# Look-up inputs by halves of the batch and two broadcast loads for the dense rows, in a one-core recommendation tower

## The chip, the core and the metric

The kernel runs on one core of a Trainium2 chip. The metric is the device time of one execution in microseconds, the median over runs. The core has a matrix engine (TensorE, PE in the rows), VectorE (DVE), ScalarE (ACT), GpSimd (POOL) and SyncE (SP), each with a program of its own; they wait for one another on semaphores. SyncE issues nearly all transfers, GpSimd the gathers, and all of them share 16 DMA engines.

## The reference

For 2048 rows the reference looks up 16 embeddings of 16 values in tables of 1,000 to 125,000 rows, forms products with 39 x 16 context values per row (r_x0), and contracts them with weights into z (16 x 16 values per row). A three-layer network follows.

```python
e = stack([tbl_s[ids[:, s]] for s in range(16)], axis=1)      # 2048 x 16 x 16
A = repeat(x0, s, axis=1)                                     # n = 16 * 39 pairs
Bm = repeat(xl, f, axis=2).reshape(b, s * f, d)               # xl is e
z = einsum('bnh,bnd,nk,khd,kd->bkh', A, Bm, alpha, w, hv)
h = concatenate([z, dense_ctx], axis=1)                       # 256 + 16 values
h = maximum(h @ W_top1 + b_top1, 0); h = maximum(h @ W_top2 + b_top2, 0)
y = h @ W_top3
```

## The kernel before, in words

**Look-ups.** Seven of the sixteen tables are gathered from memory by GpSimd (L340, indirect transfers of 128 rows each). The nine small ones (ONE_HOT, 1,000 or 1,250 rows) lie on chip and are looked up by matmuls. A row number is split in a low digit (0 to 249) and a high digit (0 to 3 or 4). `find_digits` computes both, ScalarE stores the low digits to the scratch tensor low_dram (L387), and SyncE's `load_low` brings them back broadcast to all 128 partitions in low_h. `make_onehot` (DVE) compares them with each partition's number, two instructions for one table, one for each half of the 250 low digits. `look_up` (PE) multiplies the one-hots with the table, which `split_tables` has split in three bf16 parts, into one of two banks of PSUM. `pick_rows` (DVE) masks the right high digit and sums, two instructions, into e_all. A unit is one table for one quarter of the batch (512 rows): 4 x 9 = 36 units, numbered i = 9u + n for quarter u and table n. Quarter 0 is looked up before the main loop, the others inside it.

**Main loop.** Eight groups of 256 rows, each with NC = 5 steps; step number = 5g + c. In each step DVE multiplies a 128 x 2048 block of x0 (x_main for steps c = 0 to 3, x_last for c = 4) with the spread and transposed embeddings (L585), and PE contracts the product with the coefficients (`contract`, L678). ScalarE spreads the embeddings of the next group (`spread_group`, L411), which needs all nine units of that pair of groups, and PE transposes them (L668). Inside group g PE also runs the network of group g-1: layer1 at steps c = 0 and 1 (L693, L699), layer2 at c = 2 (L709), layer3 at the end (L718).

**Order.** It is written out by hand. `units_at(step)` gives the units that are looked up in a step: UNITS_AT counts them over the ten steps of a pair of groups, and those are for the next pair. In PE's program a step is: its look-ups, its contraction, transposes and layers. In DVE's: the product, the picks of this step's units, the one-hots of the next step's. In ScalarE's program `round_dense` (which waits for all dense loads, dense_in) stands before `spread_group(0, 0)` and `copy_coef`; `split_dense` on DVE follows the ninth pick and waits for the rounding.

**Dense rows.** The 16 dense values and a row of ones (for the bias), padded to 32 rows of 2048 values, are needed four times, once for each block of 32 partitions, and w1d (32 x 512) likewise. They are staged in x0_last's second buffer and in z_sb. Before the change SyncE waits for low_in and then issues twelve transfers for them, each of 32 partitions.

**SyncE's queue before:** ids, masks, weights, alpha, mask, tables; after low_stored the first quarter of low_h (three transfers of three tables); after those have landed the dense loads; x_main and x_last of group 0; the second quarter of low_h; x_main of group 1; w1z, w2, w3; after dense_low x_last of group 1; then for each group g from 2 on, released by DVE's products of group g-2, low_h (g = 2 and 4), x_main and x_last.

Of the kernel before, what the change touches and what calls it, by code (L numbers as in the profile page):

```python
# [99 lines left out]
FIRST_COLS = COL0[3]  # L100
LAST_COEF_AT = (2, 4, 6, 8)

UNITS_AT = (2, 1, 1, 2, 1, 1, 1)
LAYER1_AT, LAYER2_AT = (0, 1), 2
# [32 lines left out]
def dlrm_tower(nc, ids, ids_d, small_tables, tables, x0_m, x0_l, dense_t, alpha, w_hv, w1z, w1d, w2, b2, w3,  # L137
               slot_mask, masks, y):
    with ExitStack() as ctx:
        def sb(name, shape, dt=F32):  # L140
            return ctx.enter_context(nc.sbuf_tensor(name, shape, dt))
# [27 lines left out]
        parts = sb("parts", [RC, PARTS, W], BF16)  # L169
        onehot = sb("onehot", [RC, NSMALL, 2, QUARTER], BF16)  # L170
        low16 = sb("low16", [P, NSMALL * TILES], F16)
        low_h = sb("low_h", [P, 2, NSMALL, QUARTER], F16)
        pick = sb("pick", [P, NSMALL * TILES, DMAX])
        picked = sb("picked", [P, 2, QT * DMAX * D])
        low_dram = nc.dram_tensor("low_dram", [NSMALL, B], F16, kind="Internal").ap()
        alpha_sb = sb("alpha_sb", [P, F8, K])
# [23 lines left out]

        dense_f = [x0_last[:, 1, :, :].rearrange("p h b -> p (h b)")[:, a * HALF:(a + 1) * HALF] for a in range(2)]
        w1d_f = z_sb[:, 0, :, :].rearrange("p a b -> p (a b)")
# [32 lines left out]
        low_stored = sem("low_stored")  # L235
        low_in = [[sem(f"low_in{u}_{i}") for i in range(NSMALL // 3)] for u in range(2)]
        pick_ready = sem("pick_ready")
# [28 lines left out]

        PREP_LOADS, MLP_LOADS, DENSE_LOADS = 2, 4, 12

# [3 lines left out]
        def _(sp):  # L272
# [6 lines left out]

            def load_low(u):  # L280

                if u >= 2:
                    sp.wait_ge(onehot_ready, 2 * NSMALL * (u - 1))
                for n in range(0, NSMALL, 3):
                    sp.dma_start(low_h[:, u % 2, n:n + 3, :], low_dram[n:n + 3, u * QUARTER:(u + 1) * QUARTER].unsqueeze(0).broadcast_to(
                        [P, 3, QUARTER])).then_inc(low_in[u % 2][n // 3], 16)

# [10 lines left out]

            for n in range(NSMALL // 3):
                sp.wait_ge(low_in[0][n], 16)  # L300
            for q in range(4):
                rows = slice(32 * q, 32 * q + 32)
                for a in range(2):
                    sp.dma_start(dense_f[a][rows, :], dense_t[:, a * HALF:(a + 1) * HALF]).then_inc(dense_in, 16)  # L304
                sp.dma_start(w1d_f[rows, :], w1d).then_inc(dense_in, 16)  # L305
            load_main(0, 0)
            load_last(0, 0)
            load_low(1)
            load_main(1, 1)
# [5 lines left out]
            for g in range(2, GROUPS):  # L315
                sp.wait_ge(product_ready, NC * (g - 2) + MC)
                if g % 2 == 0 and g // 2 + 1 < 4:
                    load_low(g // 2 + 1)
                load_main(g, g % 2)
                sp.wait_ge(product_ready, NC * (g - 1))  # L320
                load_last(g, g % 2)
# [24 lines left out]
        def _(act):  # L346
# [39 lines left out]
            act.wait_ge(low_ready, 1)  # L386
            act.dma_start(low_dram.rearrange("n b -> (n b)").rearrange("(p c) -> p c", p=P), low16[:, :]).then_inc(low_stored, 16)  # L387
            spread_weights()
# [77 lines left out]
        def _(dve):  # L466
# [57 lines left out]
            def make_onehot(i):  # L524

                n, u = i % NSMALL, i // NSMALL
                dve.wait_ge(low_in[u % 2][n // 3], 16 * (u // 2 + 1))
                if u > 0:
                    dve.wait_ge(onehot_used, i - NSMALL + 1)
                for c in range(2):  # L530
                    dve.tensor_scalar(onehot[:, n, c, :], low_h[0:RC, u % 2, n, :], low_sb[:, c:c + 1], None,  # L531
                                      ALU.is_equal).then_inc(onehot_ready, 1)
# [25 lines left out]
            split_tables(0, slice(0, FIRST_COLS))  # L558
            dve.wait_ge(split_step, 4)
            split_tables(1, slice(FIRST_COLS, W))  # L560
            make_onehot(0)
            dve.wait_ge(pick_ready, 1)
            dve.wait_ge(low_ready, 1)
            for n in range(NSMALL):
                if n < NSMALL - 1:
                    make_onehot(n + 1)
                pick_rows(n)
            split_dense()
            for i in units_at(0):
# [25 lines left out]
        def _(pe):  # L595
# [26 lines left out]
            def look_up(i):  # L622
# [3 lines left out]
                if i >= 2:  # L626
                    pe.wait_ge(picked_out, i - 1)
                pe.wait_ge(onehot_ready, 2 * (i + 1))
                for t in range(QT):
                    at = t * P  # L630
                    for c in range(2):
                        for part in range(PARTS):
                            col = COL0[n] + c * w
                            last = pe.matmul(look_ps[i % 2][:, t * w:(t + 1) * w], onehot[:, n, c, at:at + P],  # L634
                                             parts[:, part, col:col + w], start=(t == 0 and c == 0 and part == 0),
                                             stop=(c == 1 and part == PARTS - 1), skip_group_check=True)
# [154 lines left out]
```

## Time and profile before

| | |
|---|---|
| runs, us | 207.29, 205.40, 206.60 |
| median | 206.6 us |
| the profiled execution | 207.42 us, span 205.3 us |
| PE busy | 167.3 us, 81% |
| DVE busy | 154.7 us, 75% |
| ACT busy | 65.5 us, 32% |
| POOL busy | 110.4 us, 54% |
| DMA | 26.63 MB, mean 130 GB/s |
| low_h transfers | 12 of 384 KB |
| dense_t and w1d transfers | 8 of 128 KB, 4 of 64 KB |

The span is the time between the first and last thing recorded on the core. Busy time is the union of an engine's instructions. A busy PE is not a PE at its peak, since matmuls overlap. The granted clock is the share of TensorE's full 2.4 GHz that was granted; it takes two levels, 1.00 and 0.50 (1.2 GHz). The DMA share is the mean busy share of the 16 engines and can go a little over 1, since the ends of packets are modelled.

### The profile page before, as it was taken

The numbers are of one execution on the slowest core, as the hardware profiler recorded it, in microseconds if no ns is written. First come the engines' busy times: TensorE is split into PE (matmuls) and PEld (weight loads), VectorE is DVE, ScalarE is ACT, GpSimd is POOL, SyncE is SP. The second block draws the span as 40 slices with busy tenths as digits, with TensorE's granted clock in tenths as the row PEclk, the third lists the DMA queues.
The fourth block names the chain that finished last, engine by engine and source line by source line (L and its number), as shares of the span: only waits on it lengthen the run. The fifth ranks groups of instructions, "written<-read, shape, count | busy, mean of one in ns | idle before, by whom it ended". The sixth has DMA issues, their size and how long they took to land.

```text
span 205.3 us, 5116 instructions
## 1 busy us (share of the span) xinstructions
PE 167.3 (81%) x2170; PEld 123.8 (60%) x2170; DVE 154.7 (75%) x207; ACT 65.5 (32%) x203; POOL 110.4 (54%) x119
## 2 busy tenths in 40 slices
PE   0446993337667999999968999997899899899983
PEld 0446993334354866777746667775577467477671
DVE  3597699159999898998798959888989595595000
ACT  2790018502401136118111451271117318311322
POOL 4777778777777777777777777777500000000000
PEclk9995599556997999999999999999999999999999
DMA  5645589999967999960589999209721960000000
GB/s 123 180 113 131 140 210 224 200 252 203 238 142 155 178 214 182 212 121 10 108 153 211 186 205 188 55 6 200 167 61 38 228 145 2 0 3 0 3 0 2
DMA packets 14098, 26.63 MB, mean 130 GB/s; under 512 B 3932, under 2 KB 11100, under 8 KB 12028
## 3 DMA queue, kind: packets, MB, share of 16 engines
q1 hardware_dynamic: 10156, 25.22, 56.2%
q0 software_dynamic: 3632, 1.06, 4.9%
q8 instruction: 17, 0.28, 0.6%
q10 hardware_dynamic: 288, 0.04, 0.1%
q14 instruction: 5, 0.04, 0.1%
HBM read 26.26 MB, written 0.05 MB: 128 GB/s over the span
## 4 chain that ended last, share of the span: by engine, by line
PE 51%; DVE 21%; DMA 15%; issue 6%; SPq 4%; ACT 1%; DVEq 0%
PE bank L678 15%; DVE prod L585 14%; PE bank L699 13%; PE bank L709 12%; DMA low_h<-low_dram 12%; PE bank L634 5%; DVE onehot L531 4%; PE bank L668 3%; PE bank L693 2%; DMA low_dram<-low 2%; SPq L304 2%; DVE picked L543 2%; DMA prod<-ids_d 1%; SPq L305 1%; DVE prod L487 1%
## 5 line engine op out<-in xcount | busy, mean ns | idle before, releaser
L340 POOL DMA_INDIRECT e_all<-tbl,ids_sb x112 | 109.0, 973 | 35.4 <-issue 33.9
L585 DVE TENSOR_TENSOR prod<-x_main,bank 128x2048 f32<-128x2048 f32 x32 | 72.1, 2278 | 9.2 <-issue 9.2
L678 PE MATMUL bank<-prod,coef 128*32 128x256 f32 x640 | 45.0, 397 | 9.2 <-DVE prod L585 8.5
L634 PE MATMUL bank<-parts,onehot 125*128 125x80 bf16 (+1 forms) x864 | 38.5, 210 | 12.1 <-DVE onehot L531 12.1
L634 PEld LDWEIGHTS bank<-parts,onehot 125*128 125x128 bf16 x864 | 36.4, 107 | 16.9 <-issue 14.9
L411 ACT ACTIVATE spread<-e_all 128x128 f32<-128x128 f32 (+3 forms) x128 | 29.0, 331 | 12.2 <-DMA e_all<-tbl,ids_sb 11.5
L678 PEld LDWEIGHTS bank<-prod,coef 128*32 128x32 f32 x640 | 17.3, 111 | 24.3 <-DVE prod L585 11.6
L699 PE MATMUL bank<-z_sb,w1z_sb 128*128 128x256 f32 x128 | 30.4, 380 | 0.0
L709 PE MATMUL bank<-h_sb,w_sb 128*128 128x256 f32 x128 | 29.8, 386 | 0.7 <-ACT h_sb L421 0.7
L531 DVE TENSOR_SCALAR onehot<-low_h,masks_sb 125x512 bf16<-125x512 f16 x72 | 23.2, 372 | 6.7 <-DMA low_h<-low_dram 6.7
L709 PEld LDWEIGHTS bank<-h_sb,w_sb 128*128 128x128 f32 x128 | 23.7, 190 | 6.9 <-ACT h_sb L421 3.1
L421 ACT ACTIVATE h_sb<-bank 128x512 f32<-128x512 f32 x16 | 9.6, 598 | 54.7 <-PE bank L699 54.7
L699 PEld LDWEIGHTS bank<-z_sb,w1z_sb 128*128 128x128 f32 x128 | 23.1, 189 | 2.7 <-ACT z_sb L441 0.2
L543 DVE TENSOR_TENSOR picked<-bank,pick 128x320 f32<-128x320 f32 (+1 forms) x36 | 16.7, 464 | 10.0 <-PE bank L634 9.7
L668 PE MATMUL bank<-ident,spread 128*128 128x128 f32 x80 | 15.1, 310 | 4.0 <-ACT spread L411 4.0
L585 DVE TENSOR_TENSOR prod<-x_last,bank 128x2048 f32<-128x2048 f32 x8 | 18.2, 2278 | 0.0
L547 DVE TENSOR_REDUCE e_all<-picked 128x64 f32<-128x320 f32 (+1 forms) x36 | 16.7, 464 | 1.2
L668 PEld LDWEIGHTS bank<-ident,spread 128*128 128x128 f32 x80 | 9.3, 153 | 13.6 <-issue 13.6
L429 ACT ACTIVATE h_sb<-bank,b_sb 128x256 f32<-128x256 f32 x16 | 6.7, 471 | 12.9 <-PE bank L709 12.9
L435 ACT ACTIVATE y_sb<-bank 128x64 f32<-128x64 f32 x8 | 1.8, 225 | 26.3 <-PE bank L718 26.3
L441 ACT ACTIVATE z_sb<-bank 128x512 f32<-128x512 f32 x8 | 4.7, 593 | 12.3 <-PE bank L678 12.3
L601 PE MATMUL bank<-prod 128*128 128x128 f32 x10 | 2.5, 434 | 7.3 <-DVE prod L514 7.3
(41 smaller groups left out, 66.1 us busy)
## 6 DMA issues: line engine op xcount, KB each, us to landing
x_main<-x_m SPq DMA_DIRECT2D x16, 512.0 KB, 8.9
x_last<-x_l SPq DMA_DIRECT2D x8, 1024.0 KB
low_h<-low_dram SPq DMA_DIRECT2D x12, 384.0 KB, 8.3
e_all<-tbl,ids_sb POOLq DMA_INDIRECT x112
x_last<-dense_t SPq DMA_DIRECT2D x8, 128.0 KB
prod<-small_tables SPq DMA_DIRECT2D x1, 672.0 KB, 6.3
w1z_sb<-w1z SPq DMA_DIRECT2D x1, 512.0 KB, 16.7
w_sb<-w SPq DMA_DIRECT2D x1, 512.0 KB, 17.1
```

The lines of the kernel that those rows point to most:

```text
L340: pool.indirect_dma_start(out=e_all[:, t * E + s * D:t * E + (s + 1) * D], out_offset=None, in_=tables[s], in_offset=bass.IndirectOffsetOn ...
L411: last = act.activation(dst, src, ACT.Copy)
L421: act.activation(h1_sb[:, 2 * i:2 * i + 2, :], h1_ps[i][:, :].rearrange("p (a b) -> p a b", a=2), ACT.Relu).then_inc(h1_ready, 1)
L531: dve.tensor_scalar(onehot[:, n, c, :], low_h[0:RC, u % 2, n, :], low_sb[:, c:c + 1], None, ALU.is_equal).then_inc(onehot_ready, 1)
L543: dve.tensor_tensor(found, look_ps[i % 2][:, 0:QT * q * D].rearrange("p (t d q) -> p t d q", t=QT, q=q), pick[:, at:at + QT, 0:q].unsqueez ...
L547: dve.tensor_reduce(e_all[:, :].rearrange("p (t i) -> p t i", i=E)[:, u * QT:(u + 1) * QT, s * D:(s + 1) * D], found, AX_X, ALU.add).then_ ...
L585: dve.tensor_tensor(prod[:, c, :, :], x0[:, p, :, :], value_bank(g, c // 2)[:, c % 2 * GB:(c % 2 + 1) * GB].unsqueeze(1).broadcast_to([P, ...
L634: last = pe.matmul(look_ps[i % 2][:, t * w:(t + 1) * w], onehot[:, n, c, at:at + P], parts[:, part, col:col + w], start=(t == 0 and c == 0 ...
L668: last = pe.transpose(value_bank(g, i)[:, col:col + P], spread[:, p, t, c * P:(c + 1) * P], ident[:, :])
L678: last = pe.matmul(z_ps[p][32 * q:32 * q + 32, a * GB:(a + 1) * GB], coef[:, c, 4 * a + q, :], prod[:, c, 4 * a + q, :], start=(c == 0 and ...
L699: last = pe.matmul(out[a], w1z_sb[:, k, cols[a]], z_sb[:, p, k, :], start=False, stop=(k == 1), skip_group_check=True)
L709: last = pe.matmul(out[a], w2_sb[:, c, cols[a]], h1_sb[:, c, :], start=(c == 0), stop=(c == N1 // P - 1))
```

## The change

The low digits come by halves (1024 rows) instead of quarters: low_dram is laid out by half, low_h has one buffer instead of two, and one transfer brings three tables of a half to each partition as a single piece of 6 KB, where it was three pieces of 1 KB. One-hots are made by halves too: `make_onehot` does nothing for odd quarters, and 18 instructions of 1024 columns serve two quarters. `look_up` takes the right 512 of them. PREFETCH = 3: three tables' one-hots are made before the second table split, the others behind the picks. UNITS_AT has no look-up in step 0 of a pair, and two each in steps 1, 3 and 5. The dense rows come in one transfer with a broadcast source of four copies, w1d in another, and SyncE does not wait for low_in before them. The second low_h load is issued once, at g = 2.

```diff
--- before.py
+++ after.py
@@ -99,8 +99,9 @@
 RUNS = spread_runs()
 FIRST_COLS = COL0[3]
 LAST_COEF_AT = (2, 4, 6, 8)
-
-UNITS_AT = (2, 1, 1, 2, 1, 1, 1)
+PREFETCH = 3
+
+UNITS_AT = (0, 2, 1, 2, 1, 2, 1)
 LAYER1_AT, LAYER2_AT = (0, 1), 2
 
 
@@ -167,12 +168,12 @@
         block_sb, half_sb = masks_sb[:, 0:J], masks_sb[:, J:J + 4]
         low_sb, high_sb = masks_sb[0:RC, J + 4:J + 6], masks_sb[:, J + 6:J + 6 + DMAX]
         parts = sb("parts", [RC, PARTS, W], BF16)
-        onehot = sb("onehot", [RC, NSMALL, 2, QUARTER], BF16)
+        onehot = sb("onehot", [RC, NSMALL, 2, HALF], BF16)
         low16 = sb("low16", [P, NSMALL * TILES], F16)
-        low_h = sb("low_h", [P, 2, NSMALL, QUARTER], F16)
+        low_h = sb("low_h", [P, NSMALL, HALF], F16)
         pick = sb("pick", [P, NSMALL * TILES, DMAX])
         picked = sb("picked", [P, 2, QT * DMAX * D])
-        low_dram = nc.dram_tensor("low_dram", [NSMALL, B], F16, kind="Internal").ap()
+        low_dram = nc.dram_tensor("low_dram", [2, NSMALL, HALF], F16, kind="Internal").ap()
         alpha_sb = sb("alpha_sb", [P, F8, K])
         w_hv_sb = sb("w_hv_sb", [P, K * H + K])
         wh_sb = sb("wh_sb", [P, K, H])
...
@@ -264,7 +266,7 @@
         y_ready = sem("y_ready")
         stored = sem("stored")
 
-        PREP_LOADS, MLP_LOADS, DENSE_LOADS = 2, 4, 12
+        PREP_LOADS, MLP_LOADS, DENSE_LOADS = 2, 4, 2
 
         block = ctx.enter_context(nc.Block())
 
@@ -277,13 +279,14 @@
             sp.dma_start(mask_sb, slot_mask).then_inc(prep_in, 16)
             sp.dma_start(table_sb, small_tables).then_inc(table_in, 16)
 
-            def load_low(u):
-
-                if u >= 2:
-                    sp.wait_ge(onehot_ready, 2 * NSMALL * (u - 1))
+            def load_low(a):
+
+                if a > 0:
+                    sp.wait_ge(onehot_ready, 2 * NSMALL)
                 for n in range(0, NSMALL, 3):
-                    sp.dma_start(low_h[:, u % 2, n:n + 3, :], low_dram[n:n + 3, u * QUARTER:(u + 1) * QUARTER].unsqueeze(0).broadcast_to(
-                        [P, 3, QUARTER])).then_inc(low_in[u % 2][n // 3], 16)
+                    sp.dma_start(low_h[:, n:n + 3, :].rearrange("p n b -> p (n b)"),
+                                 low_dram[a, n:n + 3, :].rearrange("n b -> (n b)").unsqueeze(0).broadcast_to(
+                                     [P, 3 * HALF])).then_inc(low_in[n // 3], 16)
 
             sp.wait_ge(low_stored, 16)
             load_low(0)
@@ -296,16 +299,10 @@
                 sp.dma_start(x0_last[:, p, :, :], x0_l[g].unsqueeze(1).broadcast_to(
                     [2 * 8, J, HP * GB])).then_inc(last_in[p], 16)
 
-            for n in range(NSMALL // 3):
-                sp.wait_ge(low_in[0][n], 16)
-            for q in range(4):
-                rows = slice(32 * q, 32 * q + 32)
-                for a in range(2):
-                    sp.dma_start(dense_f[a][rows, :], dense_t[:, a * HALF:(a + 1) * HALF]).then_inc(dense_in, 16)
-                sp.dma_start(w1d_f[rows, :], w1d).then_inc(dense_in, 16)
+            sp.dma_start(dense_stage, dense_t.unsqueeze(0).broadcast_to([4, 32, B])).then_inc(dense_in, 16)
+            sp.dma_start(w1d_f, w1d.unsqueeze(0).broadcast_to([4, 32, N1])).then_inc(dense_in, 16)
             load_main(0, 0)
             load_last(0, 0)
-            load_low(1)
             load_main(1, 1)
             sp.dma_start(w1z_sb[:, :, :], w1z.rearrange("(a p) n -> p a n", p=P)).then_inc(mlp_in, 16)
             sp.dma_start(w2_sb[:, :, :], w2.rearrange("(a p) n -> p a n", p=P)).then_inc(mlp_in, 16)
@@ -314,8 +311,8 @@
             load_last(1, 1)
             for g in range(2, GROUPS):
                 sp.wait_ge(product_ready, NC * (g - 2) + MC)
-                if g % 2 == 0 and g // 2 + 1 < 4:
-                    load_low(g // 2 + 1)
+                if g == 2:
+                    load_low(1)
                 load_main(g, g % 2)
                 sp.wait_ge(product_ready, NC * (g - 1))
                 load_last(g, g % 2)
@@ -384,7 +381,7 @@
                 last.then_inc(coef_done, 1)
 
             act.wait_ge(low_ready, 1)
-            act.dma_start(low_dram.rearrange("n b -> (n b)").rearrange("(p c) -> p c", p=P), low16[:, :]).then_inc(low_stored, 16)
+            act.dma_start(low_dram.rearrange("u n b -> (u n b)").rearrange("(p c) -> p c", p=P), low16[:, :]).then_inc(low_stored, 16)
             spread_weights()
             spread_sums()
 
@@ -524,11 +521,13 @@
             def make_onehot(i):
 
                 n, u = i % NSMALL, i // NSMALL
-                dve.wait_ge(low_in[u % 2][n // 3], 16 * (u // 2 + 1))
+                if u % 2 > 0:
+                    return
+                dve.wait_ge(low_in[n // 3], 16 * (u // 2 + 1))
                 if u > 0:
                     dve.wait_ge(onehot_used, i - NSMALL + 1)
                 for c in range(2):
-                    dve.tensor_scalar(onehot[:, n, c, :], low_h[0:RC, u % 2, n, :], low_sb[:, c:c + 1], None,
+                    dve.tensor_scalar(onehot[:, n, c, :], low_h[0:RC, n, :], low_sb[:, c:c + 1], None,
                                       ALU.is_equal).then_inc(onehot_ready, 1)
 
             def pick_rows(i):
@@ -557,14 +556,15 @@
             dve.wait_ge(table_in, 16)
             split_tables(0, slice(0, FIRST_COLS))
             dve.wait_ge(split_step, 4)
+            for n in range(PREFETCH):
+                make_onehot(n)
             split_tables(1, slice(FIRST_COLS, W))
-            make_onehot(0)
             dve.wait_ge(pick_ready, 1)
             dve.wait_ge(low_ready, 1)
             for n in range(NSMALL):
-                if n < NSMALL - 1:
-                    make_onehot(n + 1)
                 pick_rows(n)
+                if n + PREFETCH < NSMALL:
+                    make_onehot(n + PREFETCH)
             split_dense()
             for i in units_at(0):
                 make_onehot(i)
@@ -625,9 +625,9 @@
                 w = DIGITS[n] * D
                 if i >= 2:
                     pe.wait_ge(picked_out, i - 1)
-                pe.wait_ge(onehot_ready, 2 * (i + 1))
+                pe.wait_ge(onehot_ready, 2 * (u // 2 * NSMALL + n + 1))
                 for t in range(QT):
-                    at = t * P
+                    at = (u % 2 * QT + t) * P
                     for c in range(2):
                         for part in range(PARTS):
                             col = COL0[n] + c * w
...
@@ -765,7 +765,7 @@
     rows_to = lambda a, n: _np.concatenate([a, _np.zeros((n - a.shape[0],) + a.shape[1:], a.dtype)], 0)
     arrays = {
         "ids": flat(ids.reshape(TILES, P, S).transpose(1, 0, 2)),
-        "ids_d": flat(_np.stack([flat(hot.T).reshape(P, NSMALL * TILES),
+        "ids_d": flat(_np.stack([hot.T.reshape(NSMALL, 2, HALF).transpose(1, 0, 2).reshape(P, NSMALL * TILES),
                                  hot.reshape(TILES, P, NSMALL).transpose(1, 2, 0).reshape(P, NSMALL * TILES)], 1)),
         **{f"tbl_{s}": flat(tables[f"tbl_{s}"]) for s in GATHERED},
         "x0_m": flat(x0[:, :, 0:FM]).reshape(GROUPS, 2 * FM, HP * GB),
```

## Rows read from the trace of the kernel before

**Rows 1.** the page, busy time, share of the span and instructions of each engine

```profile
PE 167.3 (81%) x2170; PEld 123.8 (60%) x2170; DVE 154.7 (75%) x207; ACT 65.5 (32%) x203; POOL 110.4 (54%) x119
```

**Rows 2.** windows: length, busy time (instructions) by engine, granted clock, DMA share, GB/s

```profile
29.00:43.50 14.50, 5.45 (x70) 4.84 (x69) 7.49 (x14) 7.76 (x23) 11.15 (x12) 0.75 1.04 227
...
60.00:103.00 43.00, 40.14 (x520) 29.10 (x512) 38.86 (x52) 12.46 (x43) 32.60 (x35) 0.96 0.74 146
```

**Rows 3.** chain of waits, start us, us, what

```profile
11.18 9.50 DMA low_h<-low_dram
...
29.16 14.33 DMA low_h<-low_dram
```

**Rows 4.** timeline, start us, us, work, idle before it; up to the first product

```profile
30.01 2.01 ACT L394 ACTIVATE dense_sb<-x_last 128x1024 fp32r<-128x1024 f32 x2 [14.19 <-DMA z_sb<-w1d]
...
33.26 3.59 ACT L411 ACTIVATE spread<-e_all 128x128 f32<-128x128 f32 x16 [0.72 <-DVE e_all L547]
...
37.00 1.94 PE L668 MATMUL bank<-ident,spread 128*128 128x128 f32 x8 [4.03 <-ACT spread L411]
...
43.52 1.17 DVE L531 TENSOR_SCALAR onehot<-low_h,masks_sb 125x512 bf16<-125x512 f16 x4 [6.55 <-DMA low_h<-low_dram]
...
44.60 2.27 DVE L585 TENSOR_TENSOR prod<-x_main,bank 128x2048 f32<-128x2048 f32 x1
```

**Rows 5.** timeline, the start: table splits, a look-up, the last pick

```profile
9.88 0.36 DVE L503 CAST parts<-prod 125x384 bf16<-125x384 f32 x1 [1.88 <-DMA prod<-small_tables]
...
11.85 0.66 DVE L503 CAST parts<-prod 125x960 bf16<-125x960 f32 x1
...
19.70 1.44 PE L634 MATMUL bank<-parts,onehot 125*128 125x64 bf16 x24 [0.31 <-DVE onehot L531]
...
32.66 0.49 DVE L547 TENSOR_REDUCE e_all<-picked 128x64 f32<-128x320 f32 x1
```

**Rows 6.** windows, the DMA system in three stretches, the clock in a fourth

```profile
12.00:20.70 8.70, 4.70 (x129) 4.48 (x122) 7.24 (x16) 3.82 (x7) 6.82 (x7) 0.72 0.55 134
...
30.20:34.20 4.00, 2.31 (x44) 2.11 (x40) 3.62 (x8) 3.28 (x7) 2.94 (x4) 1.00 1.02 223
...
42.00:43.50 1.50, 0.00 (x0) 0.00 (x0) 0.00 (x0) 0.00 (x0) 1.19 (x2) 0.50 1.17 330
...
46.00:48.00 2.00, 2.00 (x32) 1.45 (x33) 1.97 (x4) 0.00 (x0) 1.50 (x2) 0.50 1.06 206
```

**Rows 7.** one-hots (L531): from the page, and ns min/median/max from its line

```profile
L531 DVE TENSOR_SCALAR onehot<-low_h,masks_sb 125x512 bf16<-125x512 f16 x72 | 23.2, 372 | 6.7 <-DMA low_h<-low_dram 6.7
...
L531 DVE TENSOR_SCALAR onehot<-low_h,masks_sb x72: 333/347/557, 15.8 to 148.6; 125x512 bf16<-125x512 f16 x72
```

**Rows 8.** timeline of SyncE, start us, us to issue: two early loads

```profile
1.66 0.78 SPq L275 DMA_DIRECT2D w_hv_sb<-w_hv  x1
...
3.51 0.43 SPq L278 DMA_DIRECT2D prod<-small_tables  x1
```

**Rows 9.** timeline, groups 0 and 2: a contraction, the fifth product, step 10's look-ups

```profile
46.96 1.94 PE L678 MATMUL bank<-prod,coef 128*32 128x256 f32 x16
...
61.60 2.27 DVE L585 TENSOR_TENSOR prod<-x_last,bank 128x2048 f32<-128x2048 f32 x1
...
83.40 1.57 PE L634 MATMUL bank<-parts,onehot 125*128 125x64 bf16 x48
```

**Rows 10.** timeline, DVE, first products of groups 2, 3, 4, 6 and 7

```profile
81.64 2.29 DVE L585 TENSOR_TENSOR prod<-x_main,bank 128x2048 f32<-128x2048 f32 x1 [0.94 <-issue]
...
104.92 2.28 DVE L585 TENSOR_TENSOR prod<-x_main,bank 128x2048 f32<-128x2048 f32 x1
...
122.20 2.29 DVE L585 TENSOR_TENSOR prod<-x_main,bank 128x2048 f32<-128x2048 f32 x1 [2.09 <-issue]
...
161.32 8.88 DVE L585 TENSOR_TENSOR prod<-x_main,bank 128x2048 f32<-128x2048 f32 x4 [2.06 <-issue]
...
176.56 8.88 DVE L585 TENSOR_TENSOR prod<-x_main,bank 128x2048 f32<-128x2048 f32 x4 [4.16 <-issue]
```

More of the change, by code:

```diff
@@ L199, in dlrm_tower @@
         high = early(4 * NSMALL * TILES).rearrange("p (i a c) -> p i a c", i=2, a=2)
-        dense_f = [x0_last[:, 1, :, :].rearrange("p h b -> p (h b)")[:, a * HALF:(a + 1) * HALF] for a in range(2)]
+        dense_stage = x0_last[:, 1, :, :].rearrange("p h b -> p (h b)")
+        dense_f = [dense_stage[:, a * HALF:(a + 1) * HALF] for a in range(2)]
         w1d_f = z_sb[:, 0, :, :].rearrange("p a b -> p (a b)")
@@ L235, in dlrm_tower @@
         low_stored = sem("low_stored")
-        low_in = [[sem(f"low_in{u}_{i}") for i in range(NSMALL // 3)] for u in range(2)]
+        low_in = [sem(f"low_in{i}") for i in range(NSMALL // 3)]
         pick_ready = sem("pick_ready")
```

## The prediction

> **What bounds the kernel now.** The page's busy shares come first [rows 1]: TensorE (PE) 81%, VectorE (DVE) 75%. The average hides stages, so the next view is busy time by stretch [rows 2]. From 60 to 103 us PE is busy 40.14 of 43.00 us and DVE 38.86: PE sets the pace and DVE is close behind. From 29.00 to 43.50 little is computed (PE 5.45 of 14.50 us) while the DMA share is 1.04. The chain of waits tells why [rows 3]: the first low_h values take 9.50 us to land, the dense loads go out only then, and the second quarter of low_h, queued behind 2 MB of x0, is a link of 14.33 us right before the first product. The timeline gives the other paths into that product [rows 4]: ScalarE rounds the dense rows from 30.01, spreads group 0 from 33.26, PE transposes from 37.00 for 1.94. All but low_h was ready at 38.9; DVE made one-hots at 43.52 after 6.55 us of waiting, and the product started at 44.60.
>
> **Part 1, the start.** The one-hots for steps 1 to 6 exist from the start after the change, so the 14.33 us link goes, and 44.60 falls to what is late next. 38.9 would be 5.7 us gained. Two paths move it back.
>
> *The look-up path.* DVE now makes three pairs of one-hots between the two table splits. Before, the second split began at 11.85, two casts of 0.66 and two subtractions of about 1.2 [rows 5], 3.7 us, and the one-hots followed. Now DVE stands at 11.85 until the first low_h transfer lands: 0.79 MB from about 12.0 on at 330 GB/s [rows 6] is 2.4 us, with 0.6 to land 15.0. So 3.1 us of idleness precede the table work. A one-hot over 1024 rows isn't shown. It lies between 0.37 us (as one of 512) and 0.74 (twice that) [rows 7]. Two casts of 384 and 960 elements took 0.36 and 0.66 us [rows 5], which makes a fixed part of 0.16; the shortest form's 0.333 us leaves 0.17 for 512 elements, so 0.50 for 1024, and 0.45 if consecutive ones overlap by some 0.05. I take 0.475. Six of them end at 17.9, the split at 21.6. Nine picks (two instructions of up to 0.49 [rows 5], 0.95 each) and six more pairs (0.95 each) are 14.3 us: 35.9, against 33.15 before. Spread and transposes add 3.6 and 1.94: a product at about 41.5.
>
> *The dense path.* Twelve transfers of 32 rows become two whose outermost count is the four copies. Behind dense_in stand, in ScalarE's order, rounding, the spread of group 0 (and with it PE's transposes) and the coefficients' copy; DVE's split_dense needs 3.9 us after the rounding and is over sooner than these. From the start of rounding to the transposes' end it is 38.94 - 30.01 = 8.9 us, 0.7 of them a wait for picks [rows 4], so 8.2. The new transfer goes out behind all of low_h, now 2.36 MB: 7.1 us at 330 GB/s, 10.6 at 223 [rows 6], ending at 19.1 or 22.6. (In the same place before, 134 GB/s was all, at a DMA share of 0.55: the engines were half idle while the queue fed them pieces of 1 KB. The pieces are six times as long now, so I take the engines' rate; 134 would end at 29.6.) The trace shows no transfer with four outermost copies. The cheap end: it spreads over 16 engines as the twelve did, 1.31 MB at 223 GB/s, 5.9 us, done at 25 and hidden behind the picks. The dear end: one engine a copy. A busy engine moved 330/(16 x 1.17) = 17.6 GB/s in one stretch and 223/(16 x 1.02) = 13.7 in the other; four of them need 18.6 or 23.9 us. I take the dear shape: the copies are now the transfer's slowest step, and the one load with eight copies outermost, small as it is, took the queue 0.78 us to issue, where one of 128 rows took 0.43 [rows 8]. I take its faster rate, because four engines have fewer rivals once the others have done their share of x0. dense_in is then 19.1 + 18.6 = 37.7 and the product starts at 45.9, 1.3 us later than before.
>
> The Trainium skill (DMA: Bandwidth & Descriptors, Rules for kernel authors) speaks against this edit: an outermost dimension smaller than 16, such as a leading broadcast, confines a transfer to at most that many engines. No view of this trace shows it. By the same page's rate for one engine, about 27 GiB/s, the four would need an estimated 11.3 us and end at 30.4, hidden behind the picks.
>
> Queued behind the dense rows on those engines is x0: x_main's 1 MB at 223 GB/s ends 4.7 us after 37.7, and x_last is wanted 13 us after that product. Not late. The load of x_last for group 1 waits for dense_low, about 44, and is wanted after 75. SyncE no longer waits for low_in; that frees no byte, as the same engines carry them.
>
> **Part 2, the groups.** *Group 0* is DVE's: 44.60 to 63.87 (61.60 + 2.27 [rows 9]) is 19.3 us. Ten one-hots go, 0.37 each less 0.08 of overlap, 2.9 us, and one of six picks moves to group 1 (0.95): 15.5 left. But the look-ups of step 1 now start only behind the first contraction. At a granted clock of 0.50, the 1.2 GHz level [rows 6], that took 1.94 us [rows 9], and a look-up 1.44 [rows 5]: DVE waits some 1.5 us. Gain 2.3. *Group 1* is PE's. One look-up more costs 1.0, step 10's two (1.57 [rows 9]) move behind the contraction, some 0.4 of waits go: step 10's contraction is 3.3 us ahead, counted from the first product, its product 2.4. *Group 2*: every one-hot of the second half is now made in steps 10 to 15. From 81.64 to 104.92 [rows 10] DVE had 23.3 us, 2.2 of them idle. Eight pairs at 0.95 where six took about 4.1 us are +3.5, a pick less is -1.0, and half of the idle time absorbs the rest: +1.2. *Group 3* has a look-up more, +1.0, so 0.2 of the 2.4 is left. *Groups 4 and 5* lose their one-hots. They took 39.1 us, 122.20 to 161.32; two groups without look-ups are 2 x 15.24 (161.32 to 176.56 [rows 10]), and with nine look-ups of 0.9 PE's floor is 38.6. I count 1.0 gained. Groups 6 and 7: nothing. Sum: -1.2.
>
> **Sum.** +1.3 - 1.2 = +0.1 us on the profiled execution's own 207.42 (span 205.3). That execution is 0.8 above the median of 206.6, so the forecast is 206.7: no change. 1% is about what a measurement of this kernel can tell from none; its bounds are 204.5 and 208.7.
>
> **Rivals.**
> *The dense rows stay off the path*: all 16 engines carry them, or four at over 23 GB/s each. The first product is then the look-up path's, 41.5, -3.1 and with the groups -4.3: 202.3. For it: the rates above are those of 16 engines together, four alone may be faster. Against: x0 is queued beside them. It holds if dense_in is before 33.
> *The dense rows come at the crowded rate*: 22.6 + 23.9 = 46.5, first product 54.7, +10.1 - 1.2: 215.5; half way, 211. For it: x0 traffic ran at 13.7 GB/s an engine [rows 6], and 3 MB of x0 are queued beside. It makes the kernel slower from dense_in = 40 on.
> *One-hots at double price*: 0.74 for 0.475 in the 16 of steps 10 to 14 is 4.3 us on a DVE that sets the pace there: 211. Against it stands the casts' fixed part; it decides from 0.60 us each.
>
> **Chances.** Forecast's case 0.35, dense off the path 0.30, crowded rate 0.23, double price 0.12. Faster by over 1%: 0.28 of the first rival, 0.03 of the forecast, 0.31. Within 1%: 0.29 of the forecast and 0.05 at the borders, 0.34. Slower: 0.03 + 0.20 + 0.12 = 0.35. Range 201.5 to 213.5: the first rival and a microsecond of the groups below it, up to most of the way to the crowded end. The forecast case alone is 205 to 209, dense_in from 36 to 40.
>
> **What would show it.** Right: ScalarE idle until about 38, released by the dense or w1d load; a DMA share near a quarter where those run alone; first product at 46; a DVE wait in step 1; no one-hots between 46 and 80; DVE without rest from step 10 to 14. Wrong: rounding before 33 (first rival) or after 40 (second), a one-hot over 0.60 us (third). All of it fails if PE's granted clock falls where it did not before: a look-up at the lower level took 1.44 us where two took 1.57 at the upper.

## The result, and the profile after

| | kernel before | changed kernel |
|---|---|---|
| median, us | 206.94 | 217.13 (216.39 to 218.85) |
| profiled execution, us | 207.42 | 217.17 |
| span, us | 205.3 | 215.4 |

The ratio of the times is 1.053, 95% interval 1.043 to 1.063: slower by 5%. Ratios here and below leave out the slow runs (208.89 us of the kernel before, 199.88 of e8, 201.69 of e9), so they are not exactly the quotients of the medians. The forecast was no change, 206.7, and the time lies outside the range of 201.5 to 213.5.

The page of the changed kernel, busy time, share and instructions by engine, and the one-hots (compare [rows 1, 7]):

```profile
PE 165.5 (77%) x2170; PEld 124.3 (58%) x2170; DVE 148.3 (69%) x171; ACT 65.1 (30%) x203; POOL 113.0 (52%) x119
...
L530 DVE TENSOR_SCALAR onehot<-low_h,masks_sb 125x1024 bf16<-125x1024 f16 x36 | 15.8, 492 | 2.9 <-DMA low_h<-low_dram 2.9
```

The engines have no more to do than before: PE 1.8 us less, DVE 6.4 us less, and only GpSimd is busy 2.6 us longer with as many instructions. The shares of PE and DVE fell, and the span grew. The place shows in the timeline up to the first product (answering [rows 4]):

```profile
14.12 2.52 DVE L530 TENSOR_SCALAR onehot<-low_h,masks_sb 125x1024 bf16<-125x1024 f16 x6 [2.94 <-DMA low_h<-low_dram]
...
38.02 0.49 DVE L546 TENSOR_REDUCE e_all<-picked 128x64 f32<-128x320 f32 x1
...
50.45 2.00 ACT L391 ACTIVATE dense_sb<-x_last 128x1024 fp32r<-128x1024 f32 x2 [34.55 <-DMA z_sb<-w1d]
...
52.88 3.58 ACT L408 ACTIVATE spread<-e_all 128x128 f32<-128x128 f32 x16
...
56.61 1.94 PE L668 MATMUL bank<-ident,spread 128*128 128x128 f32 x8 [17.49 <-ACT spread L408]
...
57.84 4.48 DVE L585 TENSOR_TENSOR prod<-x_main,bank 128x2048 f32<-128x2048 f32 x2 [1.03 <-PE bank L668]
```

ScalarE stood idle for 34.6 us until the dense rows and w1d were there at 50.4. The ninth pick, the line at 38.02, had ended at 38.5. From the rounding on, the chain is the one forecast: 6.2 us to the transposes, 1.2 to the first product at 57.84, 13.2 us later than before.

The same kernel's windows: length, busy times, granted clock, DMA share, GB/s (answering [rows 6]):

```profile
16.00:18.00 2.00, 1.93 (x37) 1.76 (x34) 1.97 (x4) 0.00 (x0) 1.70 (x2) 1.00 1.06 383
...
20.00:22.00 2.00, 1.31 (x25) 1.32 (x25) 1.97 (x6) 0.00 (x0) 1.70 (x2) 1.00 1.06 229
...
24.00:26.00 2.00, 2.00 (x34) 2.00 (x32) 1.54 (x5) 0.00 (x0) 1.51 (x2) 1.00 1.02 129
...
40.00:42.00 2.00, 0.00 (x0) 0.00 (x0) 0.00 (x0) 0.00 (x0) 1.39 (x3) 0.50 0.98 93
...
54.00:56.00 2.00, 0.00 (x0) 0.00 (x0) 1.97 (x3) 2.00 (x11) 1.70 (x2) 0.50 0.30 87
```

Four things are to be seen. From 12 to 18 us low_h comes in its 6 KB pieces at 341 GB/s (299 to 383 in windows of 2 us), where the old pieces ran at 134 in that place [rows 6]. From 18 to 22 the rate is what x0 had before. From 24 to 42 the share stays near 1, so every DMA engine has a packet in hand nearly all the time, and yet only 93 to 163 GB/s move. From 50 to 58 the share is 0.26 to 0.34 at 72 to 98 GB/s: with the gathers, that is the work of four or five engines out of sixteen. SyncE's queue shows the same jam, start us, us to issue (e1, without it, issued these x_main loads in 1.24 us):

```profile
17.11 10.36 SPq L296 DMA_DIRECT2D x_main<-x_m  x2
...
30.73 13.42 SPq L308 DMA_DIRECT2D w_sb<-w  x1
```

The products of groups 2, 4, 6 and 7 (answering [rows 10]):

```profile
91.98 2.29 DVE L585 TENSOR_TENSOR prod<-x_main,bank 128x2048 f32<-128x2048 f32 x1 [2.06 <-issue]
...
132.97 4.49 DVE L585 TENSOR_TENSOR prod<-x_main,bank 128x2048 f32<-128x2048 f32 x2 [2.29 <-issue]
...
171.44 8.88 DVE L585 TENSOR_TENSOR prod<-x_main,bank 128x2048 f32<-128x2048 f32 x4 [2.25 <-issue]
...
186.69 8.88 DVE L585 TENSOR_TENSOR prod<-x_main,bank 128x2048 f32<-128x2048 f32 x4 [4.16 <-issue]
```

From the first product to group 6's it is 113.6 us, against 116.7 before: 3.1 gained in the groups. +13.2 and -3.1 make the +10.1 by which the span grew.

### The profile page after: what moved, and what is told of

It reads as the page before. It is cut to its first block, busy times and chain, and to the rows that moved or that the text cites. A ratio compares the mean times of both kernels' runs of the same rounds, so it can differ in the third digit from the quotient of the medians.

```text
span 215.4 us, 5046 instructions
## 1 busy us (share of the span) xinstructions
PE 165.5 (77%) x2170; PEld 124.3 (58%) x2170; DVE 148.3 (69%) x171; ACT 65.1 (30%) x203; POOL 113.0 (52%) x119
## 4 chain that ended last, share of the span: by engine, by line
PE 47%; DVE 19%; POOL 17%; issue 12%; ACT 3%; DMA 2%; DVEq 0%; POOLq 0%
POOL e_all L337 17%; DVE prod L585 16%; PE bank L678 14%; PE bank L699 12%; PE bank L709 9%; PE bank L634 7%; PE bank L668 3%; PE bank L693 2%; ACT spread L408 2%; DMA ids_sb<-ids 1%; DVE onehot L530 1%; DVE picked L542 1%; PE bank L718 0%; ACT dense_sb L391 0%; ACT h_sb L426 0%
## 5 line engine op out<-in xcount | busy, mean ns | idle before, releaser
L337 POOL DMA_INDIRECT e_all<-tbl,ids_sb x112 | 111.6, 996 | 35.8 <-issue 33.8
L678 PE MATMUL bank<-prod,coef 128*32 128x256 f32 x640 | 43.7, 391 | 10.1 <-DVE prod L585 10.0
L668 PE MATMUL bank<-ident,spread 128*128 128x128 f32 x80 | 14.6, 303 | 17.5 <-ACT spread L408 17.5
L542 DVE TENSOR_TENSOR picked<-bank,pick 128x320 f32<-128x320 f32 (+1 forms) x36 | 16.7, 463 | 14.0 <-PE bank L634 13.7
L585 DVE TENSOR_TENSOR prod<-x_last,bank 128x2048 f32<-128x2048 f32 x8 | 18.2, 2278 | 0.0
L530 DVE TENSOR_SCALAR onehot<-low_h,masks_sb 125x1024 bf16<-125x1024 f16 x36 | 15.8, 492 | 2.9 <-DMA low_h<-low_dram 2.9
L391 ACT ACTIVATE dense_sb<-x_last 128x1024 fp32r<-128x1024 f32 x2 | 2.0, 1048 | 34.6 <-DMA z_sb<-w1d 34.6
L470 DVE TENSOR_TENSOR dense_sb<-x_last,dense_sb 64x1024 fp32r<-64x1024 f32 x2 | 2.4, 1220 | 14.5 <-ACT w1d_sb L392 14.5
```

Of the source, the lines that this page charges most:

```text
L337: pool.indirect_dma_start(out=e_all[:, t * E + s * D:t * E + (s + 1) * D], out_offset=None, in_=tables[s], in_offset=bass.IndirectOffsetOn ...
L530: dve.tensor_scalar(onehot[:, n, c, :], low_h[0:RC, n, :], low_sb[:, c:c + 1], None, ALU.is_equal).then_inc(onehot_ready, 1)
L542: dve.tensor_tensor(found, look_ps[i % 2][:, 0:QT * q * D].rearrange("p (t d q) -> p t d q", t=QT, q=q), pick[:, at:at + QT, 0:q].unsqueez ...
L585: dve.tensor_tensor(prod[:, c, :, :], x0[:, p, :, :], value_bank(g, c // 2)[:, c % 2 * GB:(c % 2 + 1) * GB].unsqueeze(1).broadcast_to([P, ...
L668: last = pe.transpose(value_bank(g, i)[:, col:col + P], spread[:, p, t, c * P:(c + 1) * P], ident[:, :])
L678: last = pe.matmul(z_ps[p][32 * q:32 * q + 32, a * GB:(a + 1) * GB], coef[:, c, 4 * a + q, :], prod[:, c, 4 * a + q, :], start=(c == 0 and ...
```

## The experiments

Ratios are to the kernel before, with their 95% intervals. Where no ratio is given, the time is that of a single run.

### Is it the four outermost copies? (e1 to e4)

e1 puts the twelve transfers back into the changed kernel, with no wait before them:

```diff
-sp.dma_start(dense_stage, dense_t.unsqueeze(0).broadcast_to([4, 32, B])).then_inc(dense_in, 16)
-sp.dma_start(w1d_f, w1d.unsqueeze(0).broadcast_to([4, 32, N1])).then_inc(dense_in, 16)
+for q in range(4):
+    rows = slice(32 * q, 32 * q + 32)
+    for a in range(2):
+        sp.dma_start(dense_f[a][rows, :], dense_t[:, a * HALF:(a + 1) * HALF]).then_inc(dense_in, 16)
+    sp.dma_start(w1d_f[rows, :], w1d).then_inc(dense_in, 16)
```

> The changed kernel with the dense rows and w1d in twelve transfers of 32 rows again, still without SyncE's wait before them. Theory 1 (the four outermost copies hold those 1.31 MB on four engines): they spread over all engines, dense_in comes at 25 to 28 instead of 50.2, the first product at about 42 instead of 57.84, and the time falls by 13 to 16 us to 201 to 204. Theory 2 (the place is what hurts: behind all 2.36 MB of low_h, with x0 right behind them): the twelve are as late as the two, 214 to 217. Theory 3 (the new schedule of one-hots and look-ups costs the time): no more than 3 us come back.

Measured: 199.61 us, 0.973 (0.966 to 0.980). The rounding starts at 26.72 and the first product at 39.82. The timeline of e1:

```profile
26.72 2.00 ACT L394 ACTIVATE dense_sb<-x_last 128x1024 fp32r<-128x1024 f32 x2 [10.68 <-DMA z_sb<-w1d]
...
34.87 3.59 ACT L411 ACTIVATE spread<-e_all 128x128 f32<-128x128 f32 x16 [5.63 <-DVE e_all L549]
...
39.82 4.49 DVE L588 TENSOR_TENSOR prod<-x_main,bank 128x2048 f32<-128x2048 f32 x2 [1.25 <-PE bank L671]
...
71.37 3.60 ACT L411 ACTIVATE spread<-e_all 128x128 f32<-128x128 f32 x16 [2.95 <-DMA e_all<-tbl,ids_sb]
...
75.78 2.29 DVE L588 TENSOR_TENSOR prod<-x_main,bank 128x2048 f32<-128x2048 f32 x1 [3.69 <-issue]
```

The whole loss and more comes back, 17.5 us between the medians and about 16.5 by the two ratios: theory 1, and against theories 2 and 3. The time is a little below the expected range. What remains of the change is a gain of 2.7%. The spread of group 0 now waits for the picks, as the forecast's look-up path had it. In the profiled execution (201.93 us, the longest of the four) the first product is 18.0 us earlier than in the changed kernel, and the span only 15.3 us shorter: 1.8 us of the rest went before group 2, whose spread waited for the gathers.

e2 is the converse: the two transfers in the kernel before, its wait kept.

> The kernel before with the two transfers of four copies in place of the twelve, nothing else changed (SyncE's wait stays). Theory 1: the load takes over 20 us instead of 9, dense_in moves from 30.0 to about 45 to 52, the first product from 44.6 to 53 to 60, the time to 215 to 222. Theory 2: in their old place the two cost nothing, 205 to 208. Theory 3: 205 to 208 as well.

Measured: 225.32 us, 1.096 (1.091 to 1.101), beyond the expected range; rounding at 49.58, first product at 61.31. The transposes ended at 57.7, so it is not the dense rows that release this product. The second quarter of low_h is held up behind them, 18 us to issue and landed at 60. The timeline of e2:

```profile
60.26 1.14 DVE L529 TENSOR_SCALAR onehot<-low_h,masks_sb 125x512 bf16<-125x512 f16 x4 [4.34 <-DMA low_h<-low_dram]
```

So the two transfers do harm in either kernel, and in this one most of all through the load queued behind them.

e3 stores the rows four times over in memory, so that source and destination are both 128 rows:

```diff
-sp.dma_start(dense_stage, dense_t.unsqueeze(0).broadcast_to([4, 32, B])).then_inc(dense_in, 16)
+sp.dma_start(dense_stage, dense_t).then_inc(dense_in, 16)     # dense_t is 128 rows now, w1d likewise
```

> The changed kernel, its dense rows and w1d stored in memory four times over, so that each of the two transfers is 128 rows to 128 partitions without a broadcast; the same bytes in as many transfers. Theory 1: 128 rows spread over 16 engines, so it is as fast as with twelve transfers, within 1% of e1, 201 to 204, and SyncE's issuing is not held up. If large single transfers were the harm, and not the outermost count, it would stay at 214 to 217.

Measured: 201.41 us, 0.979 (0.972 to 0.985), intervals overlapping with e1's. The rounding starts at 25.33, 1.4 us earlier than in e1, and the first product at 42.37, 2.5 later: in that execution TensorE's granted clock was 0.50 from 20 to 36 us, where e1 had 1.00, and the last pick ended at 37.3. A large single transfer is no harm.

e4 holds x0 back:

```diff
+sp.wait_ge(dense_in, 16 * DENSE_LOADS)
 load_main(0, 0)
```

> The changed kernel with SyncE waiting for the dense rows and w1d before it issues x0. Theory 1: from about 18 us on the DMA share is near 0.25 and the rate about 100 GB/s (four engines at the 25 GB/s that the last stretch of the changed kernel shows for them), 1.31 MB take about 13 us, dense_in comes at 31 to 32, x0 after it, and the first product at about 42; 203 to 207. A rival in which 16 engines carry them and are slowed by something else: share near 1 and dense_in before 25, or share near 1 and still late.

Measured: 209.52 us. The windows of e4:

```profile
18.00:20.00 2.00, 0.00 (x0) 0.00 (x0) 1.93 (x3) 0.00 (x0) 1.53 (x2) 1.00 0.42 82
...
24.00:26.00 2.00, 2.00 (x34) 2.00 (x32) 1.54 (x5) 0.00 (x0) 1.69 (x2) 1.00 0.34 65
...
30.00:32.00 2.00, 1.81 (x48) 1.68 (x49) 1.97 (x5) 0.00 (x0) 1.39 (x3) 1.00 0.33 87
```

The DMA queues of e4 from 20 to 36 us, packets, MB, share of 16 engines (q1 carries SyncE's transfers, q0 the gathers):

```profile
q1 hardware_dynamic: 215, 1.08, 24.1%
q0 software_dynamic: 373, 0.10, 6.7%
```

Alone, the two transfers keep the share at about 0.31, gathers included, and 0.24 without them: what four engines of sixteen give when they never rest. The trace does not number the engines. The rival in which sixteen are kept busy and slowed is out. But the two took from about 18.2 to 37.6, 19.4 us and not 13, 17 GB/s an engine. dense_in and the time missed the expectation; the first product came at 46.4, now waiting for x_main. Sending x0 only afterwards is still about 7 us faster than sending it beside.

### The count of outermost rows (e5 to e7)

The bytes are again stored four times over, now with a row of padding behind each block, so that the outermost dimension of the source stays 4, 8 or 16:

```diff
-sp.dma_start(dense_stage, dense_t.unsqueeze(0).broadcast_to([4, 32, B])).then_inc(dense_in, 16)
+sp.dma_start(dense_stage, dense_t[:, 0:32, :]).then_inc(dense_in, 16)   # [4, 33, B]; e6 [8, 17, B]; e7 [16, 9, B]
```

> The changed kernel, its dense rows and w1d stored four times over with one row of padding behind each copy, so that the transfers keep an outermost count of four (4 x 32 rows) but every copy reads memory of its own. Theory 1 (the outermost count puts them on four engines): as slow as the change, dense_in at 45 to 51, 214 to 218. A rival inside it, that the copies collide because they read the same addresses: dense_in before 38, 204 to 208, although four engines carry them.

> As the one with four, but laid out as 8 x 16 rows with padding, the same bytes. Theory 1: eight engines carry them, half the bytes each, about 14 to 17 us beside x0 instead of 32: dense_in at 32 to 36, first product at 40 to 44, 200 to 206. If any outermost step that is not the 128 rows in one run were the harm: as with four.

> As 16 x 8 rows with padding. Theory 1: sixteen engines, dense_in at 24 to 27, the same time as with plain rows within 1.5%, 199 to 204. The series 4, 8, 16 falls with the count; if the padding or the shape were the cause, the three would be alike.

| outermost count | time, us | rounding starts, us | first product, us |
|---|---|---|---|
| 4 (e5) | 219.07 | 52.23 | 59.59 |
| 8 (e6) | 213.88 | 40.77 | 48.12 |
| 16 (e7) | 201.01 | 27.32 | 40.55 |

The series falls with the count, as theory 1 says, and the rival is out: four copies that read memory of their own are no faster. Sixteen came out as expected. Four was about 1 us beyond its ranges, and eight was clearly slower than expected: rounding at 40.8 for 32 to 36, and 213.9 us for 200 to 206. Its windows and those of four and sixteen, the same stretch of each (e5, e6, e7):

```profile
22.00:30.00 8.00, 8.00 (x92) 8.00 (x93) 6.32 (x16) 0.00 (x0) 6.00 (x6) 1.00 1.06 135
```

```profile
22.00:30.00 8.00, 8.00 (x93) 8.00 (x93) 6.32 (x16) 0.00 (x0) 6.00 (x6) 1.00 1.08 120
```

```profile
22.00:30.00 8.00, 8.00 (x91) 8.00 (x89) 6.69 (x16) 2.52 (x3) 6.17 (x7) 1.00 1.04 221
```

All three have every DMA engine busy. With sixteen 221 GB/s move, with four 135, with eight 120. So beside x0 such a transfer does not only use few engines: all of them move less while it lasts.

### What is left to gain (e8 to e12)

e8 is e1 with UNITS_AT = (2, 1, 1, 2, 1, 1, 1).

> The changed kernel with twelve dense transfers, and the look-ups dealt to the steps as before (two in step 0). Theory 1 puts 3 us gained on the groups down to one-hots that are gone from the first half, not to the dealing: within 1% of e1, 199 to 202. If the dealing made the gain, 2 to 3 us are lost, 202 to 203; if the look-ups of step 1 behind a contraction at the lower clock cost 1.5 us, as in my prediction, it is 1 us faster than e1.

Measured: 199.01 us, 0.965 (0.957 to 0.972). The intervals of e1 and e8 overlap, so the dealing is worth nothing certain; the gain is not its doing.

e9 is e1 with `if g == 3: load_low(1)` for `if g == 2`.

> The changed kernel with twelve dense transfers; SyncE issues the second half of low_h at g = 3 instead of g = 2. Theory: with the dense rows off the path, the next limit is GpSimd's gathers, whose landing for group 2 lags 8.9 us behind while low_h and x0 are moving (ScalarE waits 2.95 us for them at 71.4, DVE 3.7 us at 75.8). With low_h out of their way the wait shrinks by 2 to 3 us, and the time falls to 197 to 199, if low_h still lands before step 10's one-hots. Against it: low_h then lands late, and DVE waits for it: 200 to 204.

Measured: 198.81 us, 0.959 (0.951 to 0.967). ScalarE's spread of group 2 starts at 67.94 without a wait, where e1 stood until 71.37, and group 2's product at 73.78, 2.0 earlier:

```profile
67.94 3.63 ACT L411 ACTIVATE spread<-e_all 128x128 f32<-128x128 f32 x16
```

That the second half of low_h was in the way of the gathers is not shown by this. With low_h at g = 2 the same spread waited 2.95 us for gathers in e1 and 3.70 in e8, but 0.55 in e10 and not at all in e12:

```profile
69.62 3.63 ACT L413 ACTIVATE spread<-e_all 128x128 f32<-128x128 f32 x16
```

So the wait differs that much between executions and variants without the move. Of the five variants e9 has the lowest ratio; its interval overlaps e1's (0.966 to 0.980) and just misses e12's.

e10 makes the table split first and the one-hots behind it.

> The changed kernel with twelve dense transfers, and the first three tables' one-hots made behind the second table split instead of ahead of it. My prediction charged the order of the change with 3 us of DVE idleness (2.4 in e1's trace). If that sets the first product, it comes 2 us earlier (about 37.8 for 39.8), and 0 to 2 us of it reach the end, since the gathers bind at group 2: 198 to 200. If PE's half clock in that stretch sets it, no change, 199 to 201.

Measured: 199.74 us, 0.969 (0.962 to 0.975); first product at 38.87, 1.0 earlier and not the 2 expected, since the spread of group 0 now waits for its gathers until 33.9, and group 1's at 57.84, the same as e1's: the spread of group 1 waits for its gathers until 50.5 in both. The idle 2.4 us of DVE were worth nothing clear of noise.

e11 joins e8, e9 and e10.

> Twelve dense transfers, the old dealing of units to steps, low_h's second half at g = 3, the table split ahead of the one-hots: everything that seems to help together. If the gains add, 195 to 197.5; if the gathers bind whatever is done before them, 197.5 to 199.5.

Measured: 198.94 us, 0.961 (0.954 to 0.968). They don't add; it stands with e9. Both beat the kernel before by 4%.

e12 is e1 with SyncE's wait for low_in restored.

> The changed kernel with twelve dense transfers and SyncE's wait for all of low_h before them, as in the kernel before. It prices the wait that the change took away: dense_in moves from 26.7 to about 29 to 31, still before the picks end at 34.8, so the first product stays at 40 and the time within 1% of e1, 198.5 to 201.5. If x0's later issue mattered, 202 or more.

Measured: 201.18 us, 0.976 (0.968 to 0.985), rounding at 29.48. The wait was nearly free, as expected.

### What stretches 19 us to 32 (e13 to e16)

In each of these SyncE issues a part of x0 behind the two transfers of four copies and waits for dense_in before the rest.

> The changed kernel, SyncE issues only x_main of group 0 (1 MB, to partitions 0 to 63 and then 64 to 127) behind the two dense transfers and waits for these before the rest of x0. The dense rows took 32 us beside all of x0 and 18 alone. If the loss comes from whatever moves at the same time (theory 1a), 1 MB beside them makes it 20 to 25 us: dense_in at 39 to 43. If one kind of load collides with them and the other does not (theory 1b), this one or e14 stays at 18 to 20 us and the other is near 25 or more.

> As e13, but with x_last of group 0 (1 MB to all 128 partitions, sixteen rows read by eight partitions each) beside the dense rows instead of x_main. Theory 1a: the same as e13 within 2 us. Theory 1b: one of the two is at 18 to 20 us, the other at 25 or more.

> The changed kernel, SyncE issues x_main and x_last of group 0 (2 MB) behind the two dense transfers, and waits for these before the rest. One kind alone, 1 MB, cost the dense rows nothing to speak of (dense_in 37.8 and 38.6 against 37.6). If the two kinds in flight together slow the engines (theory 1c), dense_in comes at 43 or later and the rate falls to 120 to 160 GB/s for some 10 us. If only the amount counts (theory 1d, nothing until the third MB), 38 to 40.

> As e15, but with x_main of groups 0 and 1 (2 MB of one kind) beside the dense rows, x_last after them. Theory 1c: 38 to 40, as with 1 MB. Theory 1d: the same as e15. If this one is late too, at 43 or more, and e15 as well, two MB of anything do it.

| beside the dense rows | rounding starts, us | time, us | kernel before, run along with it, us |
|---|---|---|---|
| nothing (e4) | 37.83 | 209.52 | 205.46 |
| x_main, 1 MB (e13) | 38.06 | 206.80 | 206.22 |
| x_last, 1 MB (e14) | 38.84 | 208.02 | 206.22 |
| x_main and x_last, 2 MB (e15) | 43.76 | 210.94 | 208.02 |
| x_main twice, 2 MB (e16) | 43.31 | 210.50 | 208.02 |
| all: 3 MB of x0, w1z and w2 (changed kernel) | 50.45 | 217.13 | 206.94 |

The first megabyte costs at most 1.0 us, whatever it is; the second 5 to 6, whatever it is; the rest, a third megabyte and the weights, another 7. That is against 1a (some loss from the first on), against 1b and against 1c (the kinds). 1d had nothing until the third, and fell too. The windows of e16 show how it looks, 24 to 26 beside 36 to 38:

```profile
24.00:26.00 2.00, 2.00 (x27) 2.00 (x24) 1.97 (x5) 0.00 (x0) 1.39 (x3) 0.50 1.06 106
...
36.00:38.00 2.00, 1.73 (x9) 1.62 (x8) 0.98 (x2) 0.00 (x0) 1.62 (x2) 0.50 0.33 74
```

From 18 to 22 us the dense rows and the first megabyte together still moved 199 to 229 GB/s (e15, e16 and the changed kernel). From about 22 on all DMA engines are busy at about half that rate, in e15 and e16 until about 30, and then the share falls to that of the few. So the loss begins only when x0 beyond the first megabyte is under way beside them. Which resource they share there isn't settled; port, memory or the order in which an engine takes its queue were not told apart.

## Why the prediction was wrong, step by step

**The start's diagnosis: right.** The wait for the second quarter of low_h was the bound, and without it and with a quick dense load the first product moves to 39.8 (e1; forecast 41.5 for that case). low_h ran at 341 GB/s on the mean for 330 taken and ended at about 18.2 for 19.1.

**The look-up path: right.** DVE stood 2.94 us before its first one-hots (forecast 3.1), a one-hot took 0.492 (0.475, between bounds 0.37 and 0.74), and in e1 the last pick ended at 34.8 (35.9). In the changed kernel it ended at 38.5, as PE stood 4.1 us in the middle of a look-up, behind no semaphore; dense_in hid that:

```profile
35.21 2.25 PE L634 MATMUL bank<-parts,onehot 125*128 125x80 bf16 x31 [4.13 <-issue]
```

The same wait, before the same matmul, stands in e5 (2.2 us), e6 (3.7), e15 (1.5) and e16 (1.9), and in e8 to e11 (0.7 to 1.9). Each time PE goes on 1.3 to 2.3 us after the end of a single 16 KB packet of the DMA queue named "instruction". That packet starts at 32.0 in the changed kernel and at 28.0 in e1, which has no wait. That PE waited for its own program, which came late in the same jam, fits all of this, but no run isolates it.

**The shape of the dense transfers: right.** They go as if four engines carried them: the share of 0.24 in e4 and the series e5 to e7 bear it out. The Trainium skill's rule (DMA: Bandwidth & Descriptors, Rules for kernel authors) agrees with both. The estimate by its rate for one engine, 11.3 us, doesn't: alone they took 19.4.

**The price of the dense path: wrong, and this is the step that failed.** "I take its faster rate, because four engines have fewer rivals once the others have done their share of x0": 18.6 us, dense_in at 37.7. Measured: 32 us, 18.2 to 50.4, 10 GB/s an engine. 17.6 GB/s is about what an engine does when the four are alone (17, e4). Beside x0 it is lower than either row that I bounded it with, 17.6 and 13.7. Both came from stretches in which the transfers were spread over sixteen engines, and no row of the kernel before showed few engines beside many. I took that for a share of a fixed total that could only get better with fewer in play. The term was +13.2 where I had +1.3. The second rival, 46.5 and a first product at 54.7, was the nearest and still 3.1 us short there; that its time, 215.5, comes so near to the measured 217.1 is partly luck, as the groups gained 1.9 us more than it had.

**The groups: right in sign, short in size.** -3.1 for -1.2. Groups 0 and 1: 34.1 us (57.84 to 91.98) for 37.0, -2.9 for -2.4, and in part by luck: group 0 gained 1.5 where I had 2.3, group 1 another 1.5 where I had next to nothing, with a granted clock of 1.00 for the 0.91 it had before. Groups 2 and 3: 41.0 for 40.6, +0.4 where I had +2.2. Group 2 took 24.1 for 23.3, +0.8 for +1.2, so its doubled one-hots cost about what I said; group 3 took 16.9 for 17.3, -0.4 where I had charged a look-up with +1.0, and no run says why. Groups 4 and 5: 38.5 for 39.1, -0.65 for -1.0. The third rival, one-hots at double price, didn't occur. My sum also had two slips: the terms of group 2 add up to +1.4 and not +1.2, and 1.0 gained in groups 4 and 5 is more than the 0.5 down to my own floor of 38.6. Without them the forecast is 0.7 us higher, which changes nothing.

**The chances.** The case behind the result had 0.23. I took the dear shape of the transfers and then their cheap rate, and the forecast stood or fell with both. Had the rate's lower end been half of the worst row, since no row showed few engines among many, the dense path's end would have lain beyond the result and the range would have held it.

## What to carry to other kernels

Look at the outermost dimension of each transfer before its size: twelve transfers of 32 rows beat two whose source begins with four copies, by some 17 us here. Where the copies are wanted in one transfer, make 128 rows of it in memory (e3) or arrange sixteen blocks (e7). A transfer on few engines is worst with others queued beside it; if it can't be avoided, let no more than a megabyte go out beside it before it has finished (e13, e14; e4 sends none). And a rate read where all engines work is no floor for a stretch in which some have a transfer of their own.

## What the runs showed of the hardware

- A transfer with an outermost count of four kept the DMA share at 0.31 and moved about 75 GB/s, gathers included, 0.24 and 67 without them (e4).
- Beside it, 1 MB spread over all engines cost at most 1.0 us, 2 MB cost 5 to 6; then the share was about 1.0 and the rate 89 to 163 GB/s (e16, changed kernel), where transfers with an outermost count of sixteen or more had 221 (e7) and 227 [rows 2].
- Three rows of 1 KB or one piece of 6 KB to each partition, broadcast from memory: 134 [rows 6] against 299 to 383 GB/s (changed kernel, 12 to 18 us).
- A gather of 128 short rows took 8.9 us from issue to landing while megabytes moved on the other queue, by the chain of waits in e1; ScalarE's wait for the gathers at that place was 0 to 3.7 us in runs that load low_h at the same step.
